# Short-key attention: scores of two units as one pair on four row groups, and what that moves in four engines' queues

## The reference, cut to what matters

```
q, k, v = x @ Wq, ctx @ Wk, ctx @ Wv          # heads of 16
s       = q k^T * scale  (masked in layer 0)   # 1024 x 77 for each head
p       = softmax(s)
x      += tanh(g) * (p v) @ Wo                 # layer 0: the masked stage
```

## Time and profile before

| | us |
|---|---|
| median of 3 runs | 2650.71 (2646.29 to 2651.43) |
| profiled execution | 2645.53 |
| its span | 2643.8 |
| PE busy | 2394.4 (91%) |
| DVE busy | 1609.2 (61%) |
| ACT busy | 1298.3 (49%) |
| POOL busy | 1310.7 (50%) |

### The profile page before, as it was taken

One profiled execution on the slowest core, in us unless ns is written; L12 is line 12 of the kernel. 1 busy time (PEld: TensorE's weight loads), 2 busy tenths in 40 slices (PEclk: granted clock), 3 DMA queues, 4 the chain that ended last, 5 costly groups with the idle time before them and its releaser, 6 DMA issues. The chain is left out here.

```text
span 2643.8 us, 42280 instructions
## 1 busy us (share of the span) xinstructions
PE 2394.4 (91%) x12771; PEld 1437.0 (54%) x12787; DVE 1609.2 (61%) x3275; ACT 1298.3 (49%) x2567; POOL 1310.7 (50%) x2112
## 2 busy tenths in 40 slices
PE   6997999999996986899999999899969966999997
PEld 3554786666663553345444453455546653666664
DVE  5885674655554976777868767598866653221221
ACT  4664454444442883566666666567644421222221
POOL 3665773234445652233443535467865214656663
PEclk9998999999998997999999999999989987999999
DMA  4001000000100005131231311010013151322222
GB/s 142 6 1 54 15 0 1 1 1 1 48 1 16 1 1 128 38 91 37 62 89 33 101 49 49 25 33 17 1 34 135 49 201 29 48 45 44 48 44 28
DMA packets 86128, 115.34 MB, mean 44 GB/s; under 512 B 15480, under 2 KB 65536, under 8 KB 84272
## 3 DMA queue, kind: packets, MB, share of 16 engines
q1 hardware_dynamic: 67408, 92.65, 11.7%
q0 software_dynamic: 18528, 20.31, 4.8%
HBM read 78.01 MB, written 34.64 MB: 43 GB/s over the span
## 5 line engine op out<-in xcount | busy, mean ns | idle before, releaser
L3458 ACT ACTIVATE L2S_pT<-L2S_t_ps 128x512 f32<-128x512 f32 (+3 forms) x768 | 356.5, 491 | 221.6 <-PE L2S_t_ps L3279 213.0
L3522 DVE TENSOR_REDUCE L2S_mx<-L2S_s_ps 128x1 f32<-128x768 f32 (+7 forms) x384 | 350.2, 951 | 104.7 <-PE L2S_s_ps L3202 104.1
L3279 PE MATMUL L2S_t_ps<-L2S_q,L2S_k 98*128 98x512 bf16 (+3 forms) x768 | 249.6, 335 | 17.4 <-DMA L2S_q<-L2S_mrow 7.3
L3764 POOL TENSOR_SCALAR_AFFINE_SELECT L2S_pT<-L2S_pT 128x128 f32<-128x128 f32 x512 | 151.2, 310 | 174.0 <-ACT L2S_pT L3458 169.9
L3201 PE MATMUL L2S_s_ps<-L2S_k,L2S_q 96*128 96x512 bf16 (+3 forms) x768 | 200.0, 333 | 11.5 <-DVE L2S_mx L3522 7.6
L622 POOL TENSOR_TENSOR L_prob<-L_prob,L_rc 128x616 f32<-128x616 f32 x64 | 82.2, 1285 | 231.2 <-DVE L_rc L555 231.2
L4140 DVE TENSOR_TENSOR L3B_h<-L3B_si,L3B_u_ps 128x512 f32<-128x512 f32 x71 | 48.8, 688 | 237.0 <-PE L3B_u_ps L4083 237.0
L4057 POOL DMA_INDIRECT out<-L3B_y,L3F_rows x71 | 114.7, 1616 | 134.5 <-DVE L3B_y L4146 122.3
L3279 PEld LDWEIGHTS L2S_t_ps<-L2S_q,L2S_k 98*128 98x128 bf16 x768 | 73.0, 98 | 197.8 <-ACT L2S_pT L3458 128.4
L3379 PE MATMUL L2S_o_ps<-L2S_pT,L2S_v 128*32 128x512 f32 (+3 forms) x1536 | 166.7, 507 | 0.0
L319 PE MATMUL L_scores<-weights,L_xT 128*128 128x308 f32 x512 | 143.1, 423 | 2.3 <-ACT L_xT L442 1.6
(11 more groups left out here) (548 smaller groups left out, 5748.1 us busy)
## 6 DMA issues: line engine op xcount, KB each, us to landing
qk_parts<-L2S_part SPq DMA_DIRECT2D x84, 128.0 KB, 2.3
L2S_q<-qk_parts SPq DMA_DIRECT2D x32, 192.0 KB, 3.4
L2S_k<-qk_parts SPq DMA_DIRECT2D x30, 192.0 KB, 3.4
L2S_q<-qk_parts SPq DMA_DIRECT2D x32, 128.0 KB, 3.2
L3F_w<-in_L_gu SPq DMA_DIRECT2D x8, 512.0 KB, 7.5
weights<-in_L_w SPq DMA_DIRECT2D x8, 512.0 KB, 9.7
out<-x_sb SPq DMA_DIRECT2D x8, 512.0 KB, 4.0
expert_rows<-L_xn SPq DMA_DIRECT2D x8, 512.0 KB, 3.3
```

The lines of the kernel that those rows point to most:

```text
L3279: nc.tensor.matmul(o[:, lo:512], k6[:, q % 2, j, kt * P:(kt + 1) * P], q6[:, q % 2, c, j, lo:512], start=True, stop=True).then_inc(s["t_fu ...
L3458: nc.scalar.activation(pT[:, st % SLOTS, j, lo:512], t_ps[j % 2][:, lo:512], ACT.Exp, scale=SK).then_inc(s["exp_done"], 1)
L3522: nc.vector.tensor_reduce(dst, src, AX.X, ALU.max).then_inc(s["mx_done"], 1)
L3764: nc.gpsimd.affine_select(out=edge, in_=edge, compare_op=ALU.is_ge, fill=0.0, base=0, pattern=[[1, P]], channel_multiplier=-1).then_inc(s[ ...
```

## The change

Both stages get the same edit. Two units (both halves of one tile) become a pair. Their scores go to one set of four banks, each with both halves next to each other (2 x 154 columns); the matmuls have 32 rows each, two heads, and are placed on four row groups of the array. The masked stage writes four masks of 308 columns first. All loops go in steps of two units: PE does scores of the pair s, s+1, then turns s-4 and s-3 with the ring's pieces between them; DVE does total(s-2), unit(s), unit(s+1), the other work of u, total(s-1), the other work of u+1; ACT does exp(s-1) first, exp(s) before the second turn's copy, the normalisations at the end; POOL does divide(s-2) and divide(s-1) together and then its other work as before. `prob`, `sm` and `rc` hold six units. The ring's pieces of the masked stage are moved: the second query, the second gather and the combines come one to four steps later; `ring_uses` and `pieces` write the order. In the cross stage the second query, the gathers and the combines move likewise.

```diff
+    ROW_GROUPS, WIDE = 4, 2 * NC
+    HELD, BEHIND = 6, 4
-        S_ps = [ctx.enter_context(nc.psum_tensor(f"L0_scores{i}", [P, 2, 512], F32)) for i in range(2)]
+        S_ps = ctx.enter_context(nc.psum_tensor("L0_scores", [P, ROW_GROUPS, 512], F32))
...
+        def ring_uses(g, u):
+            uses = []
+            if g + 1 < G and u == 0:
+                uses += [("x", g + 1, dh) for dh in range(KD)]
+            if 2 <= g <= G + 1:
+                uses += {1: [("c", g - 2, 1), ("c", g - 2, 2)], 2: [("c", g - 2, 3)]}.get(u, [])
+            if g + 1 < G:
+                uses += {3: [("q", g + 1, 0)], 5: [("q", g + 1, 1)]}.get(u, [])
+            if 1 <= g <= G:
+                uses += {4: [("o", g - 1, 0)], 6: [("o", g - 1, 1)], 7: [("c", g - 1, 0)]}.get(u, [])
+            if u == 7 and g % 2 == 0 and g // 2 + 1 < B:
+                uses += [("v", g // 2 + 1)]
+            return uses
+
+        def pieces(s):
+            g, u = divmod(s, UN)
+            even, odd = ring_uses(g, u), ring_uses(g, u + 1)
+            ahead = [use for use in even if use[0] == "o"]
+            rest = even[len(ahead):]
+            return (ahead, rest + odd, []) if ahead else ([], rest, odd)
...
-                pe.wait_ge(shifted, U + 1)
-                for a in range(2):
-                    nc.tensor.matmul(S_ps[U % 2][:, a, 0:BK], identb[:], ...)
-                for a in range(2):
-                    mm = nc.tensor.matmul(S_ps[U % 2][:, a, 0:BK], qT[64 * a:64 * a + 64, g % 2, hf, i * P:(i + 1) * P],
-                                          kblk[64 * a:64 * a + 64, b % 2, hf, :, :].rearrange("p h k -> p (h k)"), start=False, stop=True)
-                mm.then_inc(s_full, 1)
+                if U:
+                    pe.wait_ge(shifted, U)
+                for j in range(ROW_GROUPS):
+                    nc.tensor.matmul(S_ps[:, j, 0:2 * WIDE], identb[:], ...)
+                for hf in range(2):
+                    for j in range(ROW_GROUPS):
+                        mm = nc.tensor.matmul(S_ps[:, j, hf * WIDE:(hf + 1) * WIDE], qT[32 * j:32 * j + 32, g % 2, hf, i * P:(i + 1) * P],
+                                              kblk[32 * j:32 * j + 32, b % 2, hf, 2 * (j % 2):2 * (j % 2) + 2, :].rearrange("p h k -> p (h k)"),
+                                              start=False, stop=True, skip_group_check=True)
+                mm.then_inc(s_full, 2)
...
+            for s in range(0, STEPS, 2):            # PE
+                ahead, middle, late = pieces(s)
+                if s < UNITS:
+                    scores(s)
+                for use in ahead:
+                    piece[use[0]](*use[1:])
+                if 0 <= s - BEHIND < UNITS:
+                    turn(s - BEHIND)
+                for use in middle:
+                    piece[use[0]](*use[1:])
+                if 0 <= s - BEHIND < UNITS:
+                    turn(s - BEHIND + 1)
+                for use in late:
+                    piece[use[0]](*use[1:])
...
             def exp(U):
-                act.wait_ge(shifted, U + 3)
+                act.wait_ge(shifted, U + 1)
...
+            for s in range(0, STEPS, 2):            # ACT
+                g, u = divmod(s, UN)
+                ahead, middle, late = pieces(s)
+                if 1 <= s - 1 < UNITS:
+                    exp(s - 1)
+                for use in ahead: ...
+                if 0 <= s - BEHIND < UNITS:
+                    turn(s - BEHIND)
+                for use in middle: ...
+                if s < UNITS:
+                    exp(s)
+                if 0 <= s - BEHIND < UNITS:
+                    turn(s - BEHIND + 1)
+                for use in late: ...
+                for v in (u, u + 1):
+                    if g + 2 < G and 3 <= v <= 6:
+                        normalise(g + 2, v - 3)
...
+            for s in range(0, UNITS + 2, 2):        # DVE
+                g, u = divmod(s, UN)
+                if s:
+                    total(s - 2)
+                if s < UNITS:
+                    unit(s)
+                    unit(s + 1)
+                others(g, u)
+                if s:
+                    total(s - 1)
+                others(g, u + 1)
...
-                if 0 <= s - 2 < UNITS:              # POOL
+                if s % 2 == 0 and 0 <= s - 2 < UNITS:
                     divide(s - 2)
+                    divide(s - 1)
                 if g + 2 < G and u == 2:
                     rstd(g + 2)
```

More of the change, by code:

```diff
@@ L757, in values, with turn_x @@
                 mm.then_inc(ring_full, 1)
-            def turn_x(g):
+            def turn_x(g, dh):
                 pe.wait_ge(xn_done, CH * (g + 1))
[L761 to L765, removed]
+                o = bank(FILL["x", g, dh])
+                for i in range(CH):
+                    mm = nc.tensor.transpose(o[:, i * P:(i + 1) * P], xn[:, i, dh * P:(dh + 1) * P], chip.ident[:])
+                mm.then_inc(ring_full, 1)
             def query(g, m):
@@ L819, in combine @@
                 mm.then_inc(ring_full, 1)
+            piece = {"x": turn_x, "q": query, "o": gather, "c": combine, "v": values}
             pe.wait_ge(identb_done, 1)
@@ L823, in _ @@
             values(0)
-            turn_x(0)
+            turn_x(0, 0)
+            turn_x(0, 1)
             query(0, 0)
             query(0, 1)
-            for s in range(UNITS + UN):
-                g, u = divmod(s, UN)
+            for s in range(0, STEPS, 2):
+                ahead, middle, late = pieces(s)
                 if s < UNITS:
                     scores(s)
[L831 to L849, removed]
+                for use in ahead:
[8 more added lines that the diff above has]
+                    piece[use[0]](*use[1:])
         @block.scalar
@@ L987, in _, with others @@
             blocks(0)
[L988 removed]
             nc.vector.memset(T_ps[96:P, (KCH - 1) * P:KCH * P], 0.0).then_inc(t_free, 1)
             masks(0)
[L991 to L996 removed]
+            def others(g, u):
                 if g + 2 < G:
@@ L1328, in _ @@
             query(0, 1)
-            for s in range(LAST):
+            for s in range(0, LAST, 2):
+                ahead, middle, late = pieces(s)
                 if s < UNITS:
                     scores(s)
-                for use in ring_uses(*divmod(s, UN)):
+                for use in ahead:
                     piece[use[0]](*use[1:])
-                if 0 <= s - LAG < UNITS:
-                    turn(s - LAG)
+                if 0 <= s - BEHIND < UNITS:
+                    turn(s - BEHIND)
+                for use in middle:
+                    piece[use[0]](*use[1:])
+                if 0 <= s - BEHIND < UNITS:
+                    turn(s - BEHIND + 1)
+                for use in late:
+                    piece[use[0]](*use[1:])
         @block.scalar
@@ L1550, in _, with others @@
             ins.then_inc(bias_done, 1)
-            for s in range(LAST):
-                g, u = divmod(s, UN)
-                if s < UNITS:
-                    unit(s)
-                if 1 <= s <= UNITS:
-                    total(s - 1)
+            def others(g, u):
                 if (g, u) in ((0, 6), (0, 7)):
@@ L1574, in _ @@
                     update(G - 1, (3, 5, 6, 7).index(u))
+            for s in range(0, LAST, 2):
+                g, u = divmod(s, UN)
+                if 0 <= s - 2 < UNITS:
+                    total(s - 2)
+                if s < UNITS:
+                    unit(s)
+                    unit(s + 1)
+                others(g, u)
+                if 0 <= s - 2 < UNITS:
+                    total(s - 1)
+                others(g, u + 1)
         @block.gpsimd
```

185 lines of the change are left out of this document (86 added, 99 removed).

## The result

The changed kernel takes 2663.1 us (median of 7 runs, 2656.1 to 2669.4), the kernel before 2649.4 in the same comparison: ratio 1.0056, 95% interval 1.0038 to 1.0073. I had forecast 2631, faster, with a range to 2658. Its profiled execution (2669.4 us, span 2667.7) is the longest of its seven runs, and the one before (span 2643.8) the shortest of its seven. So the traces differ by more (23.9 us) than the medians (13.7), and part of what lies outside the two stages is scatter between executions.

A forecast was written before the change was run, and what follows sets the result against it. PE was taken as the bound, busy 105.86 of 106.10 us in the masked stage. Masked stage -12.6 and cross stage -7.0 made -19.6: 2645.5 to 2625.9 us profiled, with 5.2 added a median of 2631, range 2604 to 2658.

The forecast's parts named there:

- The block of four row groups: PE's masks and scores of a pair, both stages: row groups run four at a time, 1.35 us with masks instead of 2.16.
- Masked steps A to D: A masked-stage group's four steps, one pair each: 5.4, 6.2, 7.2, and 5.7 or 7.7 with values; before, 26.5 us a group.
- Group 0 ... loses C's wait: -0.6: Masked stage's first group: little PE work, gains the same block but loses the third step's wait, net -0.6 us.
- Cross step A, 8.9: First step of a cross-stage group: PE's pieces add up to 8.9 us, and DVE's 6.7 hides behind them.
- 0.4 for a bank: Term in the first step of a cross-stage group: 0.4 us for a late ring bank.
- Cross groups 0 and 1, "DVE keeps going": Cross stage's first two groups, set by DVE: two waits for an exponential of about 0.9 us less, -1.7 us.
- Cross C, 6.7: Third step of a cross-stage group: 6.7 us, lengthened by the wait for POOL's rstd chain.
- own 5.0: PE's own work in the third step of a cross-stage group, without the rstd wait: 5.0 us.
- Group 7 and drain, -4.8 and -3.5: Last group and drain of each stage: 4.8 us shorter in the masked stage, 3.5 in the cross stage.
- the new wait: Third steps: ACT's normalisation waits for POOL's rstd behind the divide, delaying PE's second turn; 1.0 us masked, 1.7 cross.
- the third: Rival: slower, ACT blocked by the rstd wait in third steps; 2661 us if POOL is 2.5 us late; chance 0.18.

The follow-up runs named there:

- rstd_first: The changed kernel with POOL making the normalisation's factors ahead of the two divides of its step, in both stages: 2638.5 us, ratio 0.9957 to the kernel before.
- act_d: rstd_first with, in the last step of cross-stage groups, ACT's exp(s) and two last normalisations ahead of the dense-layer, combine and values copies: 2634.1 us, ratio 0.9945.
- tail_early: rstd_first with POOL's second bias of the last self-attention tiles also ahead of the two divides of its step, in the cross stage: 2634.1 us, ratio 0.9948.
- cross_only: The changed kernel's cross stage with the masked stage of the kernel before: 2666.2 us, ratio 1.0064 to the kernel before.
- rows64: The changed kernel with only the four row groups undone, score matmuls on 64 rows, two side by side: 2672.5 us, ratio 1.0080 to the kernel before.
- b_mid: rstd_first with the second query and dense layer between PE's two turns in the second step of cross-stage groups, ACT following: 2633.0 us, ratio 0.9948.
- combo: The changed kernel with all four orders together, those of rstd_first, tail_early, act_d and b_mid: 2633.7 us, ratio 0.9936 to the kernel before.

## Why the prediction was wrong, step by step

- **The block of four row groups: right.** 1.37 us with its masks, predicted 1.35. The Trainium skill (TensorE: Matmul & The Clock Gate, "Measured speedup vs the span model") would, by the estimate from its 3.07x in the prediction, have made it 1.5; no row here shows that loss.
- **Masked steps A to D: right.** 5.5, 6.1, 7.3 (7.6 in groups 3 and 5) and 5.6 or 7.8 against 5.4, 6.2, 7.2 and 5.7 or 7.7; ACT's wait ends 4.2 us into C as worked out. Groups 1 to 6: -6.8, predicted -7.2. Its sum has two small slips: the mean of 24.5 and 26.5 is 25.5, not 25.6 (and only two of groups 1 to 5 have values), and group 6 adds up to 22.6, not 22.7.
- **"Group 0 ... loses C's wait: -0.6": failed by 5.7 us.** ACT waits in group 0 as well, and PE has least work there. The timeline of PE in step C:

```profile
42.57 0.81 PE L807 MATMUL L_scores<-L_maskb,L_identb 128*128 128x308 bf16 x4 [2.42 <-DVE L_prob L989]
43.31 1.41 PE L811 MATMUL L_scores<-L_kblk,L_qT 32*128 32x154 f32 x16
...
48.74 1.30 PE L820 MATMUL L_turned<-ident,L_prob 128*128 128x128 f32 x5 [2.77 <-ACT L_probT L898]
49.83 3.60 PE L792 MATMUL L_ring<-L_xT,weights 128*128 128x512 f32 x4
```

and the same in `rstd_first`:

```profile
42.91 1.41 PE L811 MATMUL L_scores<-L_kblk,L_qT 32*128 32x154 f32 x16
...
46.47 0.74 PE L820 MATMUL L_turned<-ident,L_prob 128*128 128x128 f32 x5 [0.88 <-ACT L_probT L898]
47.05 1.88 PE L792 MATMUL L_ring<-L_xT,weights 128*128 128x512 f32 x4
```

  In this group the query stands behind the second turn, so the whole step waits for that turn. It starts 6.2 us into C (48.74 - 42.57); then it takes 1.1 and the query 3.4: 10.7. In `rstd_first` it starts at 4.4, takes 0.6, the query 1.7: 6.7. So of the 4.0 us between them 1.8 are the wait and 2.2 the lower clock of what follows it. The score block at 1.2 GHz costs nothing, as PE waits behind it anyway. The remaining 1.7 of the 5.7 are there without the wait: group 0 of `rstd_first` takes 23.2 us against 22.1 before, with the two gaps for DVE's subtraction. I took every PE duration at a granted clock of 1.00; that is what an engine busy in 105.86 of 106.10 us gets, and here, with gaps of 2.3 to 2.8 us, the third window above has 0.50.
- **Cross step A, 8.9: failed by 1.3 to 1.9 in groups 3 to 6, 6.4 us.** "0.4 for a bank" was the term. In group 6:

```profile
1879.85 0.71 ACT L1426 ACTIVATE L_prob<-L_prob 128x616 f32<-128x616 f32 x1
...
1880.46 0.69 ACT L1434 ACTIVATE L_probT<-L_turned 128x640 f32<-128x640 f32 x1
...
1881.04 1.09 ACT L1451 ACTIVATE weights<-weights,L_nb,L_rs 128x256 f32<-128x256 f32 x2
...
1881.29 0.74 PE L1298 MATMUL L_turned<-ident,L_prob 128*128 128x128 f32 x5 [0.69 <-ACT L_probT L1434]
...
1883.87 0.28 PE L1321 MATMUL L_ring<-L_brow,L_ones_b 128*128 128x256 bf16 x1 [0.96 <-ACT L_xT L1398]
...
1886.77 0.63 PE L1330 MATMUL L_ring<-ident,weights 128*128 128x128 f32 x4 [0.34 <-ACT weights L1410]
```

  Three waits for ACT's copies, 0.69 + 0.96 + 0.34 = 2.0 (1.4 in groups 3 and 4). Two units' pieces stand in a row now, and the copies of each stand behind two exponentials and D's normalisations. `act_d` takes 0.5 to 1.1 of it away.
- **Cross groups 0 and 1, "DVE keeps going": failed by 5.5.** Not an exponential but POOL's bias holds it, which now stands behind two divides:

```profile
1725.70 1.27 POOL L1692 TENSOR_TENSOR weights<-weights,vecs 128x512 f32<-128x512 f32 x1
...
1727.01 1.54 DVE L1572 SCALAR_TENSOR_TENSOR weights<-weights 128x512 f32<-128x512 f32 x1 [2.56 <-POOL weights L1692]
...
1729.66 0.76 DVE L1519 TENSOR_REDUCE L_sm<-L_prob 128x8 f32<-128x616 f32 x1
...
1733.75 1.41 PE L1289 MATMUL L_scores<-L_kblk,L_qT 32*128 32x154 f32 x16 [5.47 <-DVE L_prob L1514]
```

  From a wait of 2.56 on DVE comes one of 5.47 on PE, and again a block at the lower level. `tail_early` confirms it for steps A and B of group 1 (-2.7, -2.8); part comes back later.
- **Cross C, 6.7: 7.0 measured in groups 3 to 6; but two errors meet here, and the wait does not end with C.** Without the wait C takes 6.1 to 6.4 (`rstd_first`) and not its "own 5.0", so the wait costs 0.7 to 0.9 in it and not 1.7: that the total fits is luck. What I left out is the rest of its price: D of groups 2, 3 and 6 is 2.2, 1.7 and 1.5 us longer than in `rstd_first`, at a granted clock of 0.72, 0.84 and 0.80 instead of 1.00, and C of group 2 is 2.8 longer. I priced the wait in C alone and at the upper level.
- **Group 7 and drain, -4.8 and -3.5: -1.6 and -2.6 measured.** The masked stage's last scores start 15.6 us after group 7 does (15.7 predicted); the rest takes 26.4 instead of 23.5. Which of its terms is short I did not test; it is not the wait, as `rstd_first` has the same 42.0 us.
- **Outside the stages, +6.7 and +3.7.** Not predicted, and mostly not the change's. Between the stages the trace before has 1441.9 us, `cross_only`, with the old masked stage, 1442.5, and those with the new one anything from 1442.1 to 1451.8. Two parts can be told apart. From 330 to 402 us the eleven traces with the new masked stage each take 1.5 us more, and neither of the two with the old one does: that goes with the changed program, and why stays open. At one place near 810 us six of the twelve later traces, `cross_only` among them, lose 1.7 to 3.1 us and the others nothing: that does not. After the cross stage the traces scatter as well (671.4 to 677.3 us, before 673.6).

The stages were to bring -19.6 and brought +13.5 in the traces, 33 us off: 2.8 of it is the start of the masked stage (scatter), 5.7 its group 0, 5.5 the cross stage's first two groups, 4.0 its group 2, 10.6 its groups 3 to 6 (6.4 of them step A), 4.1 the two drains.

So the step that failed is the price of the new wait and of the gaps around it: the prediction had them in the C steps alone, 16 us (6 x 1.0 + 6 x 1.7), with PE at the upper clock throughout; the two experiments that remove the wait give 24.6 and 24.3. The second term that failed is the cross stage's sum, in which I had added up PE's work where ACT's copies (step A) and POOL's bias (groups 0 and 1) set the time.

Of my rivals the third has the number, 2661, but by luck: its condition, POOL later than worked out, did not come (ACT's wait ends 4.2 us into C, as in the forecast). The Trainium skill (TensorEngine Tiling (Array Packing), "PSUM Bottleneck") says that tiling leaves the evacuation of PSUM as it was. `rows64` fits it, with 33 us off PE and 9.4 off the kernel, but does not separate what DVE's reading of PSUM keeps back from what the queue waits do; with four of these gone it is 14.7.

## What to carry to other kernels

When steps are merged, list for each engine what now stands ahead of what in its queue, small chains too: here four tiny POOL instructions behind two divides instead of one cost 24.6 us, more than the 14 that the whole change lost. Price PE's work at the lower clock as well wherever the change opens gaps; here gaps of 2.1 to 4.1 us were followed by such stretches. And a saving on the busiest engine counts only up to the next one: PE at 105.86 of 106.10 us became 94.78 of 103.33.

## What the runs showed of the hardware that I had not expected

The masked stage is the same program in `rstd_first`, `tail_early`, `act_d`, `b_mid` and `combo`, and step C of its group 0 takes 6.5, 8.1, 5.3, 5.3 and 6.4 us in their traces, by where in the group the granted clock falls or rises (in the window 44 to 50 us it is 0.85 in the first, 0.65 in the second, 1.00 in the third). In the steady groups the same steps agree within 0.02 us. So in a stretch where PE has gaps, a single trace says little on a microsecond or two.

And two engines that wait for nothing of each other can still stretch each other's work: DVE's addition of 128x256 numbers in SBUF took 0.4 us alone and up to 1.4 when POOL's divide had just started, in each case ending 0.3 us after the divide. The engines' busy times do not show this.
